# An adaLN block with a mixture of experts: another order for the first head group, and another last stage

## The reference, cut to what matters

```python
mod = (silu(c) @ wmod).reshape(4, 6, 1, 512)      # sa, ca, ga, sb, cb, gb
h = layernorm(x) * (1 + ca) + sa                  # x is 4 x 1024 x 512, float32
q, k, v = split(h @ W_qkv.T); q, k = rope(q), rope(k)        # 16 heads of 32
y = softmax(causal(q @ k.T / sqrt(32))) @ v
x = x + ga * (y @ W_o.T)
h = layernorm(x) * (1 + cb) + sb
w = top-2 of sigmoid(h @ Wg.T + bias), normalised # 16 experts
x = x + gb * sum_e w_e * (silu(h @ W1[e]) @ W2[e])
```

## Time and profile before

| | us |
|---|---|
| median of three runs | 1648.39 (1647.01 to 1653.48) |
| the profiled execution, whole | 1648.23 |
| its span in the trace | 1645.6 |
| first `score_columns`, the end of the prologue | 109.68 |
| first load of the last stage | 1567.59 |
| TensorE busy | 1410.0 (86% of the span) |
| VectorE busy | 1252.1 (76%) |

### The profile page before, as it was taken

How to read it: one execution, slowest core, us unless ns; L and a number is a source line. 1 busy time by engine, 2 the same in 40 slices (tenths; PEclk the granted TensorE clock), 3 DMA queues, 4 the chain that set the end, 5 groups by cost and what they waited for, 6 DMA issues and landing times. The chain is left out here.

```text
span 1645.6 us, 27981 instructions
## 1 busy us (share of the span) xinstructions
PE 1410.0 (86%) x8713; PEld 1006.4 (61%) x8713; DVE 1252.1 (76%) x2928; ACT 792.3 (48%) x1414; POOL 733.0 (45%) x683
## 2 busy tenths in 40 slices
PE   4679998899999889999988999999973999999900
PEld 3557665566566566656655666665441999999800
DVE  3578787787778778777867877789757777777778
ACT  4324546634354663334456434445513666666622
POOL 3244355342435434243543333364425677777500
PEclk8899999999999999999999999999995999999955
DMA  6555564445355444535534453553744455445389
GB/s 220 170 162 155 153 164 112 117 123 155 104 152 159 119 117 123 156 104 143 155 104 130 131 156 91 130 138 83 279 150 167 160 185 185 142 147 172 117 327 371
DMA packets 141491, 256.14 MB, mean 156 GB/s; under 512 B 17200, under 2 KB 81200, under 8 KB 141376
## 3 DMA queue, kind: packets, MB, share of 16 engines
q1 hardware_dynamic: 113280, 178.70, 36.9%
q0 software_dynamic: 13792, 47.72, 8.6%
q10 hardware_dynamic: 14304, 28.32, 5.1%
HBM read 167.34 MB, written 85.75 MB: 154 GB/s over the span
## 5 line engine op out<-in xcount | busy, mean ns | idle before, releaser
L682 ACT ACTIVATE probs<-ring 128x1024 f32<-128x1024 f32 (+3 forms) x384 | 310.8, 812 | 188.5 <-PE ring L536 116.0
L501 PE MATMUL ring<-stack_t 96*128 96x512 f32 (+3 forms) x768 | 295.6, 409 | 18.8 <-DMA stack_t<-stack_dram 15.6
L479 PE MATMUL ring<-w_parts,h_hi 128*128 128x384 f32 x1024 | 277.0, 352 | 9.8 <-DVE neg_max L863 4.0
L866 DVE CUSTOM_DVE_ANT_0 ring<-ring,later_b 128x384 f32<-128x384 f32 (+3 forms) x512 | 247.9, 497 | 26.1 <-PE ring L501 25.1
L501 PEld LDWEIGHTS ring<-stack_t 96*128 96x128 f32 x768 | 141.1, 192 | 169.9 <-issue 61.5
L1150 POOL TENSOR_TENSOR prob_sum<-prob_sum,probs 128x1024 f32<-128x1024 f32 (+3 forms) x128 | 230.0, 1797 | 29.1 <-ACT probs L682 28.5
L1163 POOL TENSOR_TENSOR rope_a<-rope_a,rope_b 128x256 f32<-128x256 f32 x128 | 93.4, 730 | 334.6 <-DVE rope_b L936 334.5
L530 PE MATMUL ring<-stack_t 128*128 128x512 f32 (+3 forms) x768 | 210.6, 356 | 26.1 <-ACT probs L682 17.2
L479 PEld LDWEIGHTS ring<-w_parts,h_hi 128*128 128x128 f32 x1024 | 190.9, 198 | 20.0 <-issue 13.2
L863 DVE TENSOR_REDUCE neg_max<-ring 128x1 f32<-128x512 f32 x256 | 175.0, 684 | 17.1 <-PE ring L501 14.8
L479 PE MATMUL ring<-w_parts,h_lo 128*128 128x384 f32 x512 | 177.4, 346 | 0.0
(11 more groups left out here) (192 smaller groups left out, 2385.6 us busy)
## 6 DMA issues: line engine op xcount, KB each, us to landing
stack_t<-stack_dram SPq DMA_DIRECT2D x384, 128.0 KB, 3.3
stack_dram<-parts SPq DMA_DIRECT2D x64, 512.0 KB, 2.9
w_parts<-w_dram SPq DMA_DIRECT2D x96, 192.0 KB, 3.5
w_sb<-y_dram SPq DMA_DIRECT2D x32, 512.0 KB, 6.6
w_sb<-w SPq DMA_DIRECT2D x22, 512.0 KB, 5.7
x_in<-x SPq DMA_DIRECT2D x32, 256.0 KB, 3.7
x<-x SPq DMA_DIRECT2D x32, 256.0 KB, 3.7
x_dram<-x SPq DMA_DIRECT2D x32, 256.0 KB, 2.9
```

What stands on the lines that cost most here:

```text
L479: mm = nc.tensor.matmul(ring[:, BANK[use], 0:384], lhs[:, c, cols], rhs[:, c, :], start=(k == 0), stop=(k == len(products) - 1))
L501: nc.tensor.matmul(ring[:, BANK[use], 0:width], stack_t[0:MROW, i % 2, 0, h, qt * P:qt * P + P], stack_t[0:MROW, i % 2, 1, h, kc * 512:kc ...
L682: nc.scalar.activation(probs[:, step % PROBS, :, q0:QC], ring[:, bank:bank + 2, q0:QC], ACT.Exp)\
L866: nc.vector.tensor_tensor_reduce(ring[:, BANK[use], 0:width], ring[:, BANK[use], 0:width], later_b[:, QC - width:QC], -1.0, 3e38, ALU.add, ...
```

## The change

Group 0 and batch 0. The projections and turns of group 0 come two steps earlier in the numbering; as the numbering of the scores stays, they stand two steps further ahead of them. In a step, `turn` of group 0 goes behind `project` on TensorE, ScalarE and VectorE. `normalise` of tile t goes to the step of the projection of t-2, ahead of its `values_of` (`NORM_FIRST`). The weights' first split goes ahead of it. `modulation_rows` goes from step -10 to -4, its later loads from -18 to -12, the third raw weight load from -16 to -10. The loads at the start are issued in the order sa, identity, x tile 0, ca, x tile 1, constants. The two 4096-column memsets of `stack_t` go from the steps -28 and -8 to the start of GpSimd's program. The turns of group 1 (but the last) come a step later.

Last stage. All 20 remaining residual tiles are read in the expert stage, the last 12 behind slots 66, 67 and 68 (before, 8 were read there, behind slots 32 and 64). `y_pair` has 11 buffers. For ten of 32 tiles (t = 2, 5, ..., 29) ScalarE scales both rows and TensorE adds them by two products with the identity into PSUM (`sum_ps`, two banks); VectorE then has two operations. `out` of tile t is issued behind the ScalarE work of tile t+3 (before, t+2).

```diff
-    return STEPS * (i - 1) + 3 * t - 13 if i else 2 * t - 30
+    return STEPS * (i - 1) + 3 * t - 13 if i else 2 * t - 32
-    return project_step(G * b, t) - (4 if b else 5)
+    return project_step(G * b, t) - (4 if b else 7)
-TURN = {step + 2: it for step, it in PROJECT.items()}
+TURN = {step + (3 if it[0] == 1 and it[1] < NT - 1 else 2): it for step, it in PROJECT.items()}
-NORM_B = {step + (1 if bt[0] else 2): bt for step, bt in NORM_A.items()}
+NORM_B = {step + (1 if bt[0] else 4): bt for step, bt in NORM_A.items()}
-SPLIT = {MOD_COL: 0, -20: 1, 3: 2, 26: 3}
+NORM_FIRST = {MOD_COL - 1: 0, MOD_COL: 1} | {project_step(0, t - 2): t for t in range(2, NT)}
+SPLIT = {MOD_COL - 2: 0, -20: 1, 3: 2, 26: 3}
-LOAD_RAW = {MOD_COL: 1, -16: 2, 6: 3}
-MOD_LOAD = {-28: (GA, SB), -18: (CB, GB)}
-MOD_ROWS = -10
-FIXED = {-28 + 3 * n: (0, n) for n in range(1 + HG)} | {-8 + n: (1, n) for n in range(1 + HG)}
+LOAD_RAW = {MOD_COL: 1, -10: 2, 6: 3}
+MOD_LOAD = {-28: (GA, SB), -12: (CB, GB)}
+MOD_ROWS = -4
+FIXED = {-28 + 3 * n: (0, n) for n in range(HG)} | {-8 + n: (1, n) for n in range(HG)}
...
-                    load_mod(CA)
                     for step in TIMELINE:
                         if step == FIRST_STEP + 1:
+                            load_mod(CA)
+                        if step == FIRST_STEP + 3:
...
-                        if step == MOD_ROWS + 2:
+                        if step == MOD_ROWS + 5:
...
@@ tensor
                             modulation_parts(SA)
+                            first_norm(0, 0)
                             modulation_parts(CA)
...
-                        if step in TURN:
+                        if step in TURN and TURN[step][0]:
                             turn(*TURN[step])
...
                         if step in PROJECT:
                             project(*PROJECT[step])
+                        if step in TURN and TURN[step][0] == 0:
+                            turn(*TURN[step])
@@ scalar
-                        if step in NORM_B:
+                        if step in NORM_B and NORM_B[step][0]:
                             normalise(*NORM_B[step])
...
+                        if step in NORM_FIRST:
+                            normalise(0, NORM_FIRST[step])
                         if step in PROJECT:
                             values_of(*PROJECT[step])
+                        if step in TURN and TURN[step][0] == 0:
+                            high_parts(*TURN[step])
@@ vector
                             modulation_parts(CA)
+                            low_weights(0)
                             modulation_columns()
...
                         if step in PROJECT:
                             rope(*PROJECT[step])
+                        if step in TURN and TURN[step][0] == 0:
+                            low_parts(*TURN[step])
@@ gpsimd
+                    for parity in range(2):
+                        nc.gpsimd.memset(stack_t[MROW:P, parity, 0, :, :].bitcast(u32), 0).then_inc(fixed_rows, 1)
+                        pool.wait_ge(fixed_rows, parity + 1)
                     nc.gpsimd.memset(neg_half[:, :], -0.5)
...
@@ expert stage
-            EARLY, FREED = 12, 8
+            EARLY, FREED = 12, TT - 12
             most = -(-B * L // P)
+            past = [most * (e + 1) if e < 2 else 2 * most + e for e in range(FREED // 4)]
...
-                            sp.wait_ge(w2_lo_r, most * ((t - EARLY) // 4 + 1))
+                            sp.wait_ge(w2_lo_r, past[(t - EARLY) // 4])
@@ last stage
-            DEPTH = 8
+            DEPTH = 11
+            BY_PE = [t for t in range(2, TT - 2) if t % 3 == 2]
+            nth = {t: n for n, t in enumerate(BY_PE)}
+            y_pair = [tiles[:, 2 * e:2 * e + 2, :] for tiles in (w1_tiles, w2_tiles) for e in range(E // 2, E)]
...
-                        if t >= EARLY:
-                            sp.dma_start(x_late[:, t - EARLY, :], x1_dram[t, :, :]).then_inc(late_in[k], 16)
+
+                @block.tensor
+                def _(pe):
+                    for n, t in enumerate(BY_PE):
+                        pe.wait_ge(m_a, n + 1)
+                        pe.wait_ge(m_b, t + 1)
+                        if n >= 2:
+                            pe.wait_ge(m_g, BY_PE[n - 2] + 1)
+                        for half in range(2):
+                            mm = nc.tensor.matmul(sum_ps[:, n % 2, :], ident_f[:, :], y_pair[t % DEPTH][:, half, :],
+                                                  start=(half == 0), stop=(half == 1))
+                        mm.then_inc(m_s, 1)
...
-                    for t in range(TT + 2):
+                    LAG = 3
+                    for t in range(TT + LAG):
...
+                            if t in nth:
+                                nc.scalar.activation(y_pair[k][:, 0, :], y_pair[k][:, 0, :], ACT.Copy, scale=weight[:, t, 0:1])\
+                                    .then_inc(m_a, 1)
...
+                        if t in nth:
+                            dve.wait_ge(m_s, nth[t] + 1)
+                            summed_y = sum_ps[:, nth[t] % 2, :]
+                        else:
...
+                        nc.vector.tensor_tensor(y, summed_y, gb_b[:, t // NT, :], ALU.mult).then_inc(m_g, 1)
                         dve.wait_ge(m_g, t + 1)
...
+                        nc.vector.tensor_tensor(y, y, x_early[t], ALU.add).then_inc(m_x, 1)
```

64 lines of the change are left out of this document (28 added, 36 removed).

## The result

The changed kernel takes 1642.51 us (median of 11 runs, 1637.67 to 1646.85); the kernel before, run 11 times beside it, takes 1649.86 (1645.44 to 1653.73). The ratio is 0.9945, with a 95% interval of 0.9932 to 0.9957. Forecast were 1625.5 us and a range of 1616 to 1637, so the change is faster, but by 0.55% (7 us between these medians) instead of 1.4% (23 us).

The account below looks back on a forecast made before the run. It took the prologue as bound by latency, the middle by TensorE, the last stage by VectorE and later transfers. 1648.23 - 16 (step 0) + 0.3 (expert stage) - 7 (last stage) = 1625.5 us, range 1616 to 1637.

Parts of the forecast that it names:

- The last stage: Last stage: 60.7 us of VectorE work and one 3.0 us stall at tile 2, clock 0.50; gain 7 us.
- rival (b): Last stage gives only 2 us, transfers staying at 369 GB/s or sums coming late; 1629 to 1631 us, chance 0.17.
- The Trainium skill's rule: Last stage: HBM to SBUF transfers held at about 358 GB/s a core, so it would need 70 us.
- The start: Prologue: first projection starts at 20.9 us instead of 22.85; gain taken as 2, bounds 0 and 3.5.
- The loop: Prologue, from tile to tile: a loop bound by ScalarE of 3.7 us, with TensorE's 3.2 fitting under it.
- The first scores: Prologue: the first scores start at 44.3 us instead of 46.5, with five projections behind them instead of four.
- The third wait: Prologue, score rows waiting for `stack_t`: grows from 4.79 to about 6 us, ends at 64.3 instead of 74.98.
- From there to step 0: End of the prologue: 29.5 us taken instead of 34.7, bounds 27.2 and 34.7; step 0 then 16 us earlier.
- The block that only shifts: Body: the 384 steps shift as a block, so what step 0 gains, the end gains.
- Rival (e): Body: a wait fixed in time absorbs the gain of step 0; 1641 us, chance 0.03.
- Steps 24 to 384: Body: these steps take as long as before, to a microsecond.
- Rival (a): Prologue: the parts' DRAM way takes what is saved, stall growing to 8 us, step 0 only 8 earlier; 1633, chance 0.22.

Follow-up runs that it names:

- run 11: Not a label but part of "run 11 times": the kernel before, unchanged, run 11 times beside the changed kernel; median 1649.86 us.
- no_sums: Changed kernel with no tiles summed by TensorE in the last stage, eleven buffers and early residual reads kept; 1641.54 us, ratio 0.9945 to before.
- sums_depth8: Changed kernel with eight instead of eleven buffers in the last stage, TensorE's sums and early residual reads kept; 1647.73 us, ratio 0.9985 to before.
- turn_plus2: Changed kernel with all turns of group 1 again two steps behind their projections; 1637.06 us, ratio 0.9897 to before.
- weights_later: Changed kernel with the first weight parts' write at step -6 instead of -12 and group 2's raw weights at -5 instead of -10; 1639.36 us, 0.9925 to before.
- turn_mix: Changed kernel with only the first five turns of group 1 a step later, the others as before; 1634.95 us, ratio 0.9902 to before.

## Why the prediction was wrong, point by point

**The last stage** held in every step but the clock: gain 7 (7.3), the stall at tile 2 of 3 us (3.50), from VectorE's first to last operation 63.7 (63.8), the rate near 410 (405), rival (b) refuted. The clock was named too low: 0.50 forecast, 0.63 measured, 31 us of TensorE instead of 34; it cost nothing, since no sum but the first was late. That the residual reads leave room in the expert stage held too (294.5 us from its first transposed tile to the last stage's first load before, 294.6 after).

**The Trainium skill's rule** of about 358 GB/s for transfers between HBM and SBUF ("DMA: Bandwidth & Descriptors", "Specifications") would have given 70 us here. The trace disagrees: 405 GB/s over 40 us, 409 in `no_sums`.

**The start** failed at the term "I take 2, so 20.9"; it is 22.77, gain 0.1. The bound of 0 to 3.5 held this value, the choice didn't. It was seen that tile 0's transposes stand ahead of `modulation_parts(CA)`, but not priced: TensorE waited for `x_hat` until 13.08 with the CA products behind it (they had started at 11.44), the columns took 3.58 us instead of 1.95, and `mod_col` moved from 15.73 to 19.61. What the missing second `first_norm` gives back (from `mod_col` to the first projection it is 3.2 us instead of 7.1) was used up in full. With the columns at their shorter length, as in `sums_depth8`, the gain is 1.2 us.

**The loop** of 3.7 us held (3.6). **The first scores** came at 46.36 instead of 44.3: 1.9 late from the start. The parts were issued at 35.40, the earliest piece went out at 40.01, 4.6 us later.

**The third wait** ended at 66.48 instead of 64.3: the same 2 us, carried on. It was 4.39 us, where 5 or more were forecast.

**From there to step 0** 29.5 us were taken and 33.2 came. This is the largest mis-sized term, and the step that failed is the choice of 29.5 "because the removed waits are some 8 us". The turns wait less, as forecast (3.7 us instead of 7.8), but a wait that was removed from one row came back in others: 1.94 us for `w_mod`, 1.23 for `neg_max` (the prediction expected "later waits of VectorE's queue", without a price). `turn_plus2`, which has the turns' waits back, is at step 0 as early as a changed kernel at the same clock. And 33.2 is the good case: to the exponential of step 0 it is 34.0 and 34.3 us in the first two profiles of the changed kernel, 36.1 to 37.2 in the six others of its order, and 35.5 to 35.8 in the three of before's. So in most executions this stretch gave nothing. (The bounds of this term were also added up a little wide: 64.3 with 27.2 and 34.7 is 91.5 to 99.0, not 91 to 99.5, and the measured 99.70 lies outside.) For `w_mod`, of "0 to 3 us" the 0 that was taken was the wrong end. The sum "2 MB, which is 5 us" left out the 1.5 MB of weight parts, 768 KB of raw weights and 0.5 MB of pieces that the tables put beside it; they move at 405 GB/s, as the window shows, and the second of the two reads lands 12.5 us after its issue:

```profile
80.00:87.00 7.00, 5.06 (x31) 3.27 (x33) 5.22 (x16) 0.64 (x2) 4.66 (x5) 1.00 1.02 405
```

`weights_later` shows that this is the cause of that wait, and that removing it moves it. The rule that goes with it is in the Trainium skill, "DMA: Bandwidth & Descriptors", "Queues, rings and completion order": each engine goes round the queues that have work, a packet at a time. So a transfer beside bulk ones on two other queues gets a part of each engine only. The trace agrees as far as it goes: the 512 KB of parts took 6.6 us to land beside them and 2.9 in the median of all 64. No run here shows the going round itself.

**The block that only shifts** is the second premise that failed. Rival (e), a wait of the body that takes back what step 0 gains, was given 0.03 with the words "I find no such wait". The wait was not in the trace of before, but its pieces landed there only 0.3 us ahead of their use. The change makes it a wait, by setting turn 5 of group 1 a step later (0.9 us) while the first use of its pieces stays at step 9, and the way got longer besides. That way, 8.8 to 10.2 us for group 0, was reckoned with for group 0 only; in group 1, beside the weights, it is 10.3 in before and 12.0 to 12.8 in the changed kernel. Steps 0 to 24 take 3.0 to 6.5 us more than before, with this wait and the clock that falls behind the longest of them. `turn_plus2` and `turn_mix`, which set turn 5 back, take 0.5 to 0.7 more than before there, and are 5 and 7 us faster than the change in their medians.

**Steps 24 to 384** were to take "as long as before, to a microsecond". They take 1025.8 to 1032.1 us over all profiles, the longer the more of them is at half clock (24 us of it in the shortest, 41 in the three longest): +4.1 us in the first profile of the changed kernel, +0.9, +2.2 and +0.7 in the others.

Added up for the profile: the forecast gain is 22.7 us, the measured one 10.3. Of the 12.4 missing, 6 lie in front of step 0, 3.3 in steps 0 to 24 and 4.1 in the body; the stages behind it gave 0.6 more than forecast, and 0.5 us more was gained outside the span. That the body's part is the change's isn't shown. Rival (a), given 0.22, had step 0 earlier by 8 us, close to the 8.5 of the mean, but by a stall of 8 us that isn't there: the number is right by luck. What sets how often the clock falls in an execution is open, and with it why the executions of before lie between 1645 and 1657.

## What to carry to other kernels

Where an operation is moved a step later, follow its product to its first use and reckon with every fixed way in between (here a write and a read over DRAM, 8.8 to 10.2 us in group 0 and 10.3 to 15.2 in group 1 beside the weights), also where the trace of before shows no wait: the slack is the time from the landing to the first use, here 0.3 us. Don't book a removed wait as time won before you know which wait of the same engine comes next; here 4 us less of waiting for `rope_sum` brought nothing at step 0. Price a load that is moved with everything that the schedule has in flight in its new window, not by its own bytes; where the engines are full, moving it chooses which wait grows, and the transfer to spare is the small one on a chain. And spread sums over engines only together with the buffers that the longer way holds: with eight instead of eleven the same sums brought nothing.

## What the runs showed of the hardware

Fourteen profiles have the same wait of TensorE in step 9. With the seven of 0.8 to 2.4 us the granted clock stayed at 1.0, with the seven of 2.7 to 6.7 us it fell to 0.5 at about its end, and steps 0 to 24 took 65.3 us and more with them instead of 64.4 and less. Ahead of step 0, 3.4 to 6.8 us at the lower clock went with 1.5 to 2.7 us more for the same work. No rule for the clock follows from so few. The core moved 405 and 409 GB/s between DRAM and SBUF over 40 us with loads and stores mixed. And the granted clock was 0.63 over 40 us in which TensorE was busy for 22.1, with a sum at 3.58 us at 1.2 GHz and 1.96 at 2.4 GHz, where a stretch with 6.5 busy of 15 us had been at 0.50 throughout.
